# Cross-attention on one core: the next batch's projections in the two halves of the array, with one room in PSUM

## What is computed

```python
x = layer_norm(hidden_states, ln1_w, ln1_b)
q = (x @ q_w + q_b)                       # per head: 16 wide
k = (encoder_hidden_states @ k_w + k_b)
v = (encoder_hidden_states @ v_w + v_b)
scores = einsum('bhqd,bhkd->bhqk', q, k) * scale
attn = softmax(where(mask, scores, mask_value))
out = einsum('bhqk,bhkd->bhqd', attn, v) @ cproj_w + cproj_b
hidden = out + residual
y = gelu(layer_norm(hidden, ln2_w, ln2_b) @ fc_w + fc_b)
return hidden + y @ proj_w + proj_b
```

## Time and profile before

| what | value |
|---|---|
| median of 3 runs | 765.36 us (765.35 to 768.17) |
| profiled execution | 768.76 us |
| its span | 767.0 us |
| mean granted clock of TensorE | 0.965 |
| busy: TensorE, its weight loads, VectorE, ScalarE, GpSimd | 702.5, 478.5, 371.3, 446.1, 120.9 us |
| busy share of the DMA engines, queue of SP / of ScalarE | 44.5% / 13.8% |

### The profile page before, as it was taken

One profiled execution on the slowest core, in us unless ns is written; L12 is line 12 of the kernel. 1 busy time (PEld: TensorE's weight loads), 2 busy tenths in 40 slices (PEclk: granted clock), 3 DMA queues, 4 the chain that ended last, 5 costly groups with the idle time before them and its releaser, 6 DMA issues.

```text
span 767.0 us, 16866 instructions
## 1 busy us (share of the span) xinstructions
PE 702.5 (92%) x7026; PEld 478.5 (62%) x7026; DVE 371.3 (48%) x824; ACT 446.1 (58%) x475; POOL 120.9 (16%) x90
## 2 busy tenths in 40 slices
PE   3657699899999999999999999999998978999997
PEld 3545466566656656666566566656664544597897
DVE  6643355265436534643464446534642331467663
ACT  3004366856676677567756775676566788733321
POOL 5222002200220032003201220131000600110010
PEclk9867799999999999999999999999999989999999
DMA  9787578657874788477938694878475800000000
GB/s 312 216 186 131 186 184 188 179 138 183 189 203 128 174 188 217 143 180 158 235 123 203 148 246 123 192 153 230 132 165 126 253 6 2 1 21 8 29 28 31
DMA packets 51275, 113.78 MB, mean 148 GB/s; under 512 B 7050, under 2 KB 40178, under 8 KB 49914
## 3 DMA queue, kind: packets, MB, share of 16 engines
q1 hardware_dynamic: 40700, 80.47, 44.5%
q10 hardware_dynamic: 10494, 32.17, 13.8%
HBM read 65.30 MB, written 47.06 MB: 146 GB/s over the span
## 4 chain that ended last, share of the span: by engine, by line
PE 76%; ACT 13%; DMA 5%; DVE 3%; issue 2%; ACTq 1%; DVEq 0%
PE O L1126 21%; PE S L1119 16%; ACT pr L583 11%; PE O L1056 10%; PE XB L1056 10%; PE O L1213 6%; PE S L1056 6%; DMA k_scr<-kpart 2%; DMA qst<-q_scr 2%; PE XB L1093 2%; PE XB L1153 2%; PE MB L1106 2%; DVE kpart L725 1%; DVE kpart L728 1%; DMA cols_s<-in_cols 1%
## 5 line engine op out<-in xcount | busy, mean ns | idle before, releaser
L583 ACT ACTIVATE pr<-S 128x1024 f32<-128x1024 f32 x416 | 400.6, 1024 | 188.6 <-PE S L1119 184.4
L1126 PE MATMUL O<-pr,vsl 128*17 128x256 f32 x3328 | 227.4, 388 | 1.3 <-DVE ot L790 1.3
L1119 PEld LDWEIGHTS S<-qst,kst 50*128 50x128 f32 x1664 | 117.1, 188 | 120.4 <-ACT pr L583 81.4
L1119 PE MATMUL S<-qst,kst 50*128 50x256 f32 x1664 | 171.7, 315 | 18.7 <-ACT pr L583 15.0
L1126 PEld LDWEIGHTS O<-pr,vsl 128*17 128x17 f32 x3328 | 75.3, 97 | 79.2 <-issue 17.7
L725 DVE TENSOR_SCALAR kpart<-O,cols_s 128x384 fp32r<-128x384 f32 x64 | 40.6, 635 | 120.7 <-PE O L1056 120.7
L771 DVE TENSOR_REDUCE mx<-MB 128x2 fp32r<-128x512 f32 x64 | 44.1, 690 | 79.0 <-PE MB L1106 79.0
L510 POOL CAST c_hi<-cT 128x768 fp32r<-128x768 f32 (+1 forms) x28 | 23.9, 852 | 348.0 <-DMA cT<-in_ctx_t 235.8
L1056 PE MATMUL XB<-w_hi,c_hi 128*128 128x256 f32 (+1 forms) x208 | 68.3, 328 | 2.1 <-DVE vsl L739 1.3
L739 DVE TENSOR_TENSOR vsl<-XB,rows_s 128x256 f32<-128x256 f32 (+1 forms) x104 | 43.3, 417 | 55.1 <-PE XB L1056 55.1
L1056 PE MATMUL O<-c_hi,w_hi 128*128 128x384 f32 (+1 forms) x128 | 52.6, 411 | 17.7 <-POOL c_lo L515 10.3
(11 more groups left out here) (100 smaller groups left out, 825.6 us busy)
## 6 DMA issues: line engine op xcount, KB each, us to landing
kst<-k_scr SPq DMA_DIRECT2D x59, 400.2 KB
k_scr<-kpart SPq DMA_DIRECT2D x48, 384.0 KB, 8.0
v_scr<-vsl ACTq DMA_DIRECT2D x8, 1768.0 KB, 11.9
kst<-k_scr SPq DMA_DIRECT2D x59, 200.1 KB
cT<-in_ctx_t ACTq DMA_DIRECT2D x21, 384.0 KB, 7.6
k_scr<-kpart SPq DMA_DIRECT2D x16, 449.0 KB, 7.1
q_scr<-qpart SPq DMA_DIRECT2D x16, 256.0 KB, 2.5
qst<-q_scr SPq DMA_DIRECT2D x59, 64.0 KB
```

Of the source, the lines that this page charges most:

```text
L583: nc.scalar.activation(pr[:, n % PBUF, :], S[:, 2 * (n % 2):2 * (n % 2) + 2, :] .rearrange("p a n -> p (a n)"), ACT.Exp).then_inc(s_.exp_d ...
L1119: last = nc.tensor.matmul(S[:, 2 * (n % 2) + g_, j * LQ:(j + 1) * LQ], kst[rows_, s, j, kt * P:(kt + 1) * P], qst[rows_, s, j, :], start=T ...
L1126: last = nc.tensor.matmul(O[32 * h:32 * h + VW, 0, 0:LQ], vsl[:, par, s, kt, h * VW:(h + 1) * VW], pr[:, n % PBUF, h * LQ:(h + 1) * LQ], s ...
```

## The change

1. **All units of batches 1 to 7 run in the halves.** `by_half` issues each product twice, on rows 0 to 63 and 64 to 127, into the two banks of a new room `U` (banks of `MB` and `XB`; `KB` is given up). VectorE adds the two. Transpositions are done in blocks of 64. `v_unit` holds two key tiles, so there are 7 V units. In batch 0's head K and V stay on 128 rows.
2. **One room.** All units share `U`, and one counter: each waits until the one before is emptied. In the head three rooms take turns (`S` in two halves, and `U`).
3. **One unit in each pair**: new tables; `CPROJ_AT`, `XT_AT`, `Q_AT` are 2, 3, 4.
4. **K is split on GpSimd** (`k_split`: a copy that rounds, then a subtraction) after VectorE has added the halves and the bias, so the K stores wait for `kl_done`. V's bias is added behind the attention (`bias_att`, after `turn_att`).
5. **SP's order** follows the tables; `store_v` goes to step 10 of its own batch, `load_mlp` to step 4 of batch 7; `x_normalise` to pair 0.

```diff
-K_AT = {0: (0, 0), 2: (0, 1), 4: (0, 2), 6: (0, 3), 8: (1, 0), 10: (1, 1), 12: (1, 2), 14: (1, 3)}
+K_AT = {0: (0, 0), 1: (0, 1), 5: (0, 2), 6: (0, 3), 9: (1, 0), 12: (1, 1), 14: (1, 2), 17: (1, 3)}
+V_AT = {13: 0, 18: 1, 19: 2, 22: 3, 23: 4, 24: 5, 25: 6}
+MAX_AT = {7: (0, 2, 0), 8: (0, 2, 1), 10: (0, 3, 0), 11: (0, 3, 1),
+          15: (1, 0, 0), 16: (1, 0, 1), 20: (1, 1, 0), 21: (1, 1, 1)}
+CPROJ_AT, XT_AT, Q_AT = 2, 3, 4
...
+        def room(u):
+            if u < len(HEAD_UNITS):
+                return (S[:, 0:2, :], S[:, 2:4, :], U[:])[u % 3]
+            return U[:]
...
             def store_k(b, mt, c):
-                sp.wait_ge(kb_taken, k_use(b, mt, c) + 1)
+                if b == 0:
+                    sp.wait_ge(unit_taken, k_unit_no(b, mt, c) + 1)
+                else:
+                    sp.wait_ge(kl_done, u + 1 - UK)
...
+            def k_split(b, mt, c):
+                total, high = kpart[:, i, 1, 0:n].bitcast(F32), kpart[:, i, 0, 0:n]
+                pool.wait_ge(unit_taken, k_unit_no(b, mt, c) + 1)
+                nc.gpsimd.tensor_copy(high, total).then_inc(ks_done, 1)
+                pool.wait_ge(ks_done, u + 1 - UK)
+                nc.gpsimd.tensor_tensor(kpart[:, i, 1, 0:n], total, high.bitcast(F32), ALU.subtract).then_inc(kl_done, 1)
...
             def k_evac(b, mt, c):
+                    nc.vector.tensor_scalar(total, halves[:, 0, 0:n], bk_s[:, mt:mt + 1], None, ALU.add).then_inc(k_half, 1)
+                    dve.wait_ge(k_half, u + 1 - UK)
+                    nc.vector.tensor_tensor(total, halves[:, 1, 0:n], total, ALU.add).then_inc(unit_taken, 1)
...
             def v_evac(b, i):
+                    nc.vector.tensor_copy(to, first_half).then_inc(v_half, 1)
+                    dve.wait_ge(v_half, KV * (b - 1) + i + 1)
+                    nc.vector.tensor_tensor(to, other, to, ALU.add).then_inc(unit_taken, 1)
...
             def divide(b, s):
-                    turn_att(s).then_inc(first.att_done, 1)
+                    turn_att(s).then_inc(first.att_turned, 1)
+                    dve.wait_ge(first.att_turned, (n + 1) // 2)
+                    bias_att(s).then_inc(first.att_done, 1)
...
+            def by_half(dst, w, m):
+                for i, (a, c) in enumerate(zip(w, m)):
+                    for g_ in range(2):
+                        rows_ = slice(g_ * HALF, g_ * HALF + HALF)
+                        last = nc.tensor.matmul(dst(g_), a[rows_], c[rows_], start=i == 0, stop=i == len(w) - 1)
+                return last
...
+            def room_free(no):
+                if no >= len(HEAD_UNITS):
+                    pe.wait_ge(unit_taken, no)
+                elif no >= 3:
+                    pe.wait_ge(unit_taken, no - 2)
```

More of the change, by code:

```diff
@@ L93, with unit_pairs, unit_at, k_unit_no @@
 QBLK = LQ // BLK
-HEAD_K = [(mt, c) for mt in range(2) for c in range(CH)]
-HEAD_MAX = [(s, j) for s in range(2) for j in range(NJ)]
+KV = -(-KT // 2)
+HEAD_UNITS = ["k00", "k01", "x", "k02", "q", "k03", "k10", "v0", "k11", "v1", "k12", "v2", "k13", "v3", "v4", "m00", "v5",
+              "m01", "v6", "m10", "m11"]
 class Section:
     pass
[L103 to L137, removed]
+def unit_pairs(b):
+    return sorted([p for p, (d, _, _) in MAX_AT.items() if b + d < B] + ([CPROJ_AT] if b > 0 else [])
+                  + ([XT_AT, Q_AT] + list(K_AT) + list(V_AT) if b + 1 < B else []))
+def unit_at(b, p):
+    return len(HEAD_UNITS) + sum(len(unit_pairs(i)) for i in range(b)) + sum(q < p for q in unit_pairs(b))
+UNITS_END = unit_at(B, 0)
 def pair_of(table, what):
     return [p for p, w in table.items() if w == what][0]
[L144 to L163, removed]
+def k_unit_no(b, mt, c):
+    return HEAD_UNITS.index(f"k{mt}{c}") if b == 0 else unit_at(b - 1, pair_of(K_AT, (mt, c)))
+def v_unit_no(b, i):
+    return HEAD_UNITS.index(f"v{i}") if b == 0 else unit_at(b - 1, pair_of(V_AT, i))
 def rows_use(b, s):
@@ L536, in _ @@
                 x_bias(b)
+                for mt in range(2):
+                    for c in range(CH):
+                        k_split(b, mt, c)
             pool.wait_ge(mlpw_in, 32)
@@ new lines, in xt_evac, with q_evac @@
+            def xt_evac(no):
+                dve.wait_ge(unit_ready, no + 1)
+                for k in range(KC):
+                    last = nc.vector.tensor_scalar(
+                        xT[:, k, :].rearrange("p (q g i) -> p g q i", q=QT, i=HALF),
+                        room(no)[:, :, k * P:(k + 1) * P].rearrange("p g (q i) -> p g q i", i=HALF),
+                        ln1_w[:, k:k + 1], ln1_b[:, k:k + 1], ALU.mult, ALU.add)
+                last.then_inc(unit_taken, 1)
+            def q_evac(b, no):
@@ L752, in q_evac @@
                 dve.wait_ge(some_in, 16)
-                dve.wait_ge(xb_ready, use + 1)
+                dve.wait_ge(unit_ready, no + 1)
+                halves = room(no)
                 for mt in range(2):
-                    last = nc.vector.tensor_scalar(qf[:, mt, :], XB[:, mt * LQ:(mt + 1) * LQ], bq_s[:, mt:mt + 1],
-                                                   some[:, b:b + 1], ALU.add, ALU.mult)
-                last.then_inc(xb_taken, 1)
+                    last = nc.vector.tensor_scalar(qf[:, mt, :], halves[:, 0, mt * LQ:(mt + 1) * LQ], bq_s[:, mt:mt + 1], None,
+                                                   ALU.add)
@@ L819, in divide @@
                 if n >= 2:
-                    dve.wait_ge(first.att_done, n // 2)
+                    dve.wait_ge(first.att_turned, n // 2)
                 quotient(first, n, s)
@@ L871, in ending @@
                 elif i == 3:
[L872 removed]
+                    hidden(B - 1, UNITS_END)
                 elif i == 4:
@@ L1099, in max_unit @@
+            def max_unit(b, s, j, no):
                 if j == 0:
                     pe.wait_ge(first.slot_in[s], 16 * FILLS * (b + 1))
[L1101 to L1102 removed]
+                room_free(no)
                 for q in range(QT):
[L1104 removed]
+                    for g_ in range(2):
                         rows_ = slice(g_ * HALF, g_ * HALF + MASKROW + 1)
[L1106 removed]
+                        last = nc.tensor.matmul(room(no)[:, g_, q * SAMPLE:(q + 1) * SAMPLE], query_set(rows_, s, j, q),
```

364 lines of the change are left out of this document (184 added, 180 removed).

## The result

The changed kernel takes **806.74 us** (median of 4 runs, 802.66 to 808.83), the kernel before on the same chip 766.38: a ratio of 1.052 [1.047, 1.057], 40 us slower. The forecast was 790 with a range of 755 to 808. The profiled execution took 805.93 us, its span 804.1, 37.1 longer than the span before.

The account below looks back on a forecast made before the run. TensorE alone was taken to bound a period. Batch 0 -13.5, batches 1 to 6 +2, head -1.2, MLP loads -3.5, tail +1, fills +28 and clock +12.5 gave +25 us, hence 790 us, range 755 to 808.

Parts of the forecast that it names:

- rival (c): GpSimd's splits and VectorE's divisions at pairs 1 and 14 hinder each other: +2 us a batch, 804 to 815; chance 0.08.
- batch with neither fill, clock nor `att_done` wait: Steady batch: 67.2 us of TensorE work plus 7.4 of waits, without the 1.6 for att_done.
- Where the fills are waited for: Fills (DMAs bringing a slot's keys) start late; TensorE's maximum at pair 20 waits 3 to 4 us in batches 0 to 6.
- the half products keep their rate: Unit products on TensorE: two 64-row products run side by side and cost the same as one full product.
- 0.21 us for each of 18 visits, 3.8 us a batch: TensorE units: leaving the halves for the full array and coming back costs 0.21 us, which the change saves.
- the term for the room: All units share U and wait for VectorE to empty it; with other late starts, 7.4 us a batch against 3.3.
- The wait for `att_done`, 1.6 us: Output projection at pair 2 waits 1.6 us behind pair 1's division, which gains V's bias (about 0.4).
- The clock, 2.5 us in five batches: TensorE's clock falls to about half after fill waits: 2.5 us in five of seven batches, 12.5 in all.
- Rival (a): Fills late but clock kept, waits of 1 to 4 us being too short to lower it: 765 to 779; chance 0.22.
- Batch 0, -13.5 and a late fill: Batch 0 loses its pair 3 fill wait, the low clock and an output projection: 86.0 to 72.5 us; late fill counted separately.
- Weights of the MLP, -3.5: Moving the MLP weight loads to batch 7, step 4, where K and V are long done, saves 3.5 us.
- Rival (b): Fills arrive in time, so fill and clock losses vanish: 750 us, or 757 with one us a batch of waits; chance 0.20.

Follow-up runs that it names:

- run 3: Changed kernel with the first maxima of the next batch's slots 0 and 1 three pairs later and the output projection one pair later: 744.8 us, ratio 0.967.
- Run 5: Row halves undone (products on all 128 rows) on the kernel of run 3: 757.88 us, ratio 0.989.
- run 1: Changed kernel with the maxima of the next batch's slots 0 and 1 three pairs later, K(1,3) and four V units in their places: 762.24 us, ratio 0.989.
- run 7: V's bias left out of the computation (no bias_att) on the kernel of run 1: 749.17 us, ratio 0.978.
- run 8: GpSimd's K splits left out on the kernel of run 1, VectorE writing the high part, low part left as it was: 745.78 us, ratio 0.973.

## Why the prediction was right, and where not

**The sign and the mechanism** held, and the size came out short: 790 us forecast, 806.74 measured. That is 1.3 us inside the upper end of the range, outside the forecast's own band (775 to 806), and inside that of rival (c) (804 to 815); that it fell on this side of 808 is luck. The stages of the sum can be set beside the runs:

| term, us a batch | forecast | measured |
|---|---|---|
| batch with neither fill, clock nor `att_done` wait | 67.2 + 7.4 - 1.6 = 73.0 | 72.93 (run 3) |
| time TensorE leaves fill 0, fill 1 | 13.5, 13.2 | 13.4, 16.2 less 2.6 given at pair 15 |
| waits for fills | 4.1 to 4.4 | 4.8 (batch 3: 4.44) |
| wait for `att_done` | 1.6 | 2.3 |
| clock | 2.5, in five of seven batches | 83.0 - 72.9 - 4.8 - 2.3 = 3.0 in batches 1 to 5 |
| pair with K, with V | 2.7, 3.3 | 2.71 to 2.97 (3.19 behind the query), 3.1 to 3.3 |

Where the 12 us between the forecast span (+25) and the measured one (+37.1) lie: batches 1 to 5 were to lose 36 at most (0.35 and 4.4 a batch, and all 12.5 of the clock) and lost 43.6; batch 0 was to gain 9.1 (13.5 less its fill) and gained 3.8; the rest was to gain 1.7 and gained 2.6.

**Where the fills are waited for**: the sum was right, the place not. It was to be 3 to 4 us at pair 20. The larger part is at pair 15 (2.6 to 6.3 us in batches 0 to 5; 0.7 in batch 6), since fill 0 took 16.0 us where TensorE left it 13.4; at pair 20 it is 1.4 to 2.4 us in four batches.

**Half products at full rate** (step "the half products keep their rate"): right. K's couples start 0.174 us apart, V's 0.118 (TensorE, changed kernel):

```profile
385.62 0.28 PE L1075 MATMUL U<-w_lo,c_hi 64*128 64x256 f32 x2
...
386.80 0.28 PE L1075 MATMUL U<-w_hi,c_lo 64*128 64x256 f32 x2
```

That is 386.80 - 385.62 over ten couples, and each couple loads two sets of weights. By the weight-load figure of the Trainium skill (TensorE: Matmul & The Clock Gate, LDWEIGHTS), an estimate for two loads one after the other is 0.21 us; the trace disagrees with that reading. Run 5 puts the halves at a gain.

**0.21 us for each of 18 visits, 3.8 us a batch**: right in size at four of the eight K pairs (0.17 to 0.20), wrong as a term to be added: all of them together come to 1.47 us a batch. Where the room's emptying is waited for anyway, the change of arrangement lies in the same gap; that is how I read the V pairs, five of which gain 0.07 or less. The sum came out all the same (73.0), perhaps because the same overlap sat in the term for the room and two errors cancelled. That is not shown: what each of the room's waits costs by itself was not tried.

**The wait for `att_done`, 1.6 us**: 2.28 measured. The step counted 0.4 for the bias and nothing for neighbours. The port rival (c), given 0.08, had the mechanism right at this one place: a quotient that takes 0.90 instead of 0.29 and a bias 0.94 instead of 0.35. It came beside the late fills and not in their place. Its price of 2 us a batch was fair as well: on run 1 the splits cost 2.7 us a period, clock included. Its row, 2.17 us against 0.69, was a weak support, since the instruction of 0.69 in the earlier trace rows reads PSUM and the other does not.

**The clock, 2.5 us in five batches**: this is the largest miss of the steady batches (3.0 in each of five, where 2.5 in five of seven was forecast). The step took the one row there was, a wait of 6.68 us, and allowed one fall a batch. There are two or three in each of batches 1 to 5, at waits of 1.7 us and more, dear by some 1.6 us where TensorE works through all of it (the projection 3.65 instead of 2.00) and by 1.2 us on average (five times 3.0 over 13 falls). Rival (a), fills late and clock kept, fell with it.

**Batch 0, -13.5 and a late fill**: it gained 3.8. Without late fills (run 3) it gains 11.4, so the term was 2 us too large. The step overlooked that the head's own waits for fills lower the clock: in the changed kernel it is still low after the first scores, where the kernel before had recovered. The same stretch, after and then before:

```profile
68.00:75.00 7.00, 6.52 (x56) 4.12 (x60) 2.52 (x6) 3.73 (x5) 3.96 (x5) 0.57 1.04 161
```

```profile
68.00:75.00 7.00, 5.29 (x56) 3.61 (x60) 2.40 (x7) 5.89 (x7) 1.85 (x2) 1.00 1.05 148
```

The other 7.5 us are the fill at pair 15, waited for 5.5, and the half clock of 111.6 to 118.4 us, of which 4.1 us lie behind that wait.

**Weights of the MLP, -3.5**: right. In run 3 batch 6 takes 72.96, as long as its neighbours; before it took 78.0 against 74.3. The head (-1.2, measured -0.9) and the rest behind the last exponential (+1, measured +1.1) were as forecast. That batch 7 gained 2.1 was in no term, and its cause stays open.

**Rival (b)**, fill in time and 757 us, did not happen in this kernel, but its number was a fair price for the kernel without the late fills: run 1 took 762.

## What to carry to other kernels

When a change moves a transfer's start or its consumer, write down for each transfer the time from issue to first use and the time it takes; the shortfalls here (2.6 and 1.8 us in the batch shown) cost half as much again, 7.0 us a batch for 4.8 of waiting, because TensorE's clock fell at 15 of its 16 waits of 1.4 to 6.3 us. Mend it by moving the consumer: starting the second transfer earlier only made the first one late. And judge a saving inside an engine (here 3.8 us of re-arranging) against the waits that already lie in the same gap, since only what sticks out of them counts.

## What was not expected of the hardware

A quotient of 128 elements with both inputs in SBUF took 0.50 us at pair 14, begun beside a GpSimd copy of 0.50, and 0.87 to 0.90 at pair 1, against 0.29 alone; GpSimd's own subtraction takes 0.87. At pair 2 a wait of 1.1 to 1.3 us never lowered TensorE's clock (0 of 12), one of 2.3 us did in 4 of 6 batches of run 1 and 5 of 6 of the changed kernel; in batch 7 of runs 1, 7 and 8 a stretch of 6.8 us at 1.2 GHz began 0.4 to 3.2 us behind a wait of 1.1 to 1.3. What decides stays open. Ten DMAs of one fill took 13.6 us at best, and up to 25.3 with another fill beside it.
